# Feed-forward products as 32-column matmuls, placed behind the first and second weighted sums of a burst step

## The chip, the cores and the metric

One core of one Trainium2 chip. The metric is the device time of one execution in microseconds. The engines are named as in the profile: PE (TensorE, its weight loads are PEld), DVE (VectorE), ACT (ScalarE), POOL (GpSimd) and SP (SyncE, which issues the DMAs).

## What is computed

A stack of four blocks over x of 32 items, 256 tokens and 128 features: an attention with biases, a feed-forward of two experts out of eight, an attention without biases, and the same feed-forward again. Each block is a residual on a layer norm.

```python
def _L0_ffn_ref(x, gate_w, down_w, down_b, up_w, up_b):
    pooled = x.mean(axis=1)
    gate = softmax(pooled @ gate_w.T)
    top_w, top_i = top_k(gate, 2)                       # two experts for each item
    top_w = top_w / (top_w.sum(axis=-1, keepdims=True) + 1e-08)
    Wd, bd, Wu, bu = down_w[top_i], down_b[top_i], up_w[top_i], up_b[top_i]
    h = gelu(einsum('bsd,bkcd->bksc', x, Wd) + bd[:, :, None, :])
    h = h * top_w[:, :, None, None]
    out = einsum('bksc,bkdc->bsd', h, Wu)
    return out + (top_w[:, :, None] * bu).sum(axis=1)[:, None, :]

x = x + attn_a(layernorm(x))      # 16 heads of 8 features, biases, two masked scores
x = x + ffn(layernorm(x))
x = x + attn_b(layernorm(x))      # 16 heads of 8 features
x = x + ffn(layernorm(x))
```

## The kernel before

Everything stays on the chip between the blocks. A "turn" is one item in one of the two halves of the stack, so there are 64 turns. A software pipeline runs steps n from -6 to 70, each cut into eight parts p, and every engine has its own list of work for (n, p), the functions `step` in the blocks of the engines. In step n the scores of turn n + 2 are made and their maxima found ("scores", `max_side`, L789; the maximum by DVE at L598), the scores of turn n are made again the other way round and put through the exponential ("exps", `exp_side`, L803; ACT at L669), turn n's probabilities meet the values (`weigh`, L774, four groups g of four heads, 32 columns each, which fill the 128 output partitions side by side), turn n - 1 is transposed and projected, and the norms of turns n + 5 and n - 3 are made.

The names of the lines on PE are: L898 query and key projection, L920 value projection, L910 transpose of the weighted sums, L931 transpose of o, L943 transposes of the normalised x, L959 output projection, L886 transpose of the maxima.

The feed-forward of four turns, a group, is done in one "burst step"; there are 16, listed in `BURSTS` (19, 23, 27, 31, 35, 39, 43, 47, 49, 51, 54, 56, 58, 62, 66, 70). `down` (L815) multiplies the four normalised items with their expert weights, ACT applies Gelu (L722, with a table load before it at L713, and another one back to the exponential's table before L669), `up` (L830 for the bias in three bf16 parts, L838 for the product, fp32) makes the second product, and DVE adds it to x in two halves (L629, semaphore `added`). An fp32 matmul of the program shows as two matmuls in the trace.

PE's list of a burst step, in order: part 3: scores 3, exps 2 and 3, L910, `weigh` 0; part 4: scores 4, `down`, L920; part 5: scores 5, exps 4, `up`, L931, exps 5, `weigh` 1; part 6: scores 6, L943, exps 6; part 7: scores 7, `weigh` 2, exps 7, L959; `weigh` 3 follows in part 1 of the next step.

Scores, exps, `down` and `up` share three PSUM pairs in a ring. The order in which they take them is written out by hand in `uses`: scores 3, exps 3, down, scores 4, exps 4, up, scores 5, exps 5, scores 6 and so on, and each waits in `fill_pair` until the use three places earlier has been read: by DVE's maximum for scores, by ACT's exponential for exps, by the four Gelus for down, by DVE's two adds for up. So scores 5 take the place of scores 4, exps 5 that of exps 4, scores 6 that of up. ACT's list in a burst step is: the exponential of exps 3, the Gelu's table load, four Gelus, the copy of the values (L733), the table load back, the exponential of exps 4. DVE's list in part 5 is: the maximum of scores 5, statistics (L529), the two adds, in some steps the gate's weights for a batch (L561 to L577), aggregates (L538); then the maximum of scores 6. Each engine works through its list in order.

Of the kernel before, what the change touches and what calls it, by code (L numbers as in the profile page):

```python
# [13 lines left out]
P = 128  # L14
ITEMS, TOKENS, WIDTH = 32, 256, 128
TILES = TOKENS // P
# [20 lines left out]
GROUP = 4  # L37
DEEP = 2 * GROUP
GROUPS, PER_GROUP = 4, 4
SHARES, IN_SHARE = 2, 2  # L40
SUMS = HEAD + 1

# [13 lines left out]
def build(nc, x_dram_in, attn_w, attn_b, gate_w, down_w, down_b, up_w, up_b, tail_c, ident_c, iota_c, pick_c, out):  # L56
    ctx = ExitStack()
    with ctx:
        def sb(name, shape, dt=FP32):
            return ctx.enter_context(nc.sbuf_tensor(name, shape, dt))  # L60

        def sem(name):
            return ctx.enter_context(nc.semaphore(name))
# [3 lines left out]
        normT = sb("normT", [P, ITEMS, TOKENS])  # L67
# [58 lines left out]
        biasu_parts = [sb(f"biasu_parts{i}", [3 * ITEMS, WIDTH], BF16) for i in range(2)]  # L126
        pick = sb("pick", [3 * ITEMS, ITEMS], BF16)
        index = [sb(f"index{i}", [1, DEEP * TOP], U32) for i in range(2)]
        wd = [sb(f"wd{i}", [P, TOP, HIDDEN]) for i in range(DEEP)]
        wu = [sb(f"wu{i}", [P, WIDTH]) for i in range(DEEP)]  # L130
        hT = [sb(f"hT{i}", [P, TOKENS]) for i in range(GROUP)]
# [82 lines left out]
        def tensor_opening(pe):  # L214
            pe.wait_ge(weights_ready, 1)
# [14 lines left out]
        for group, burst in enumerate(BURSTS):  # L230
            for j in range(GROUP):
                turn = group * GROUP + j
# [11 lines left out]
        def group_at(n):  # L244

            return BURSTS.index(n) if n in BURSTS else None
# [10 lines left out]
        def live(turn):  # L257

            return 0 <= turn < TURNS
# [25 lines left out]
        down_done, h_ready = sem("down_done"), sem("h_ready")  # L285
# [19 lines left out]
        def fill_pair(pe, *use):  # L305

            if place[use] < 3:
                return
            kind, of, p = uses[place[use] - 3]
            if kind == "scores":  # L310
                pe.wait_ge(max_done, of * PAIRS + p + 1)
            elif kind == "exps":
                pe.wait_ge(exp_done, of * PAIRS + p + 1)
            elif kind == "down":
                pe.wait_ge(h_ready, (of + 1) * GROUP)
            else:
                pe.wait_ge(added, (of + 1) * 2)
# [18 lines left out]
        with nc.Block() as block:  # L336
# [424 lines left out]
            def _(pe):  # L761
                tensor_opening(pe)

                def weigh(turn, g):

                    pe.wait_ge(exp_done, turn * PAIRS + PER_GROUP // 2 * (g + 1))
                    if g == 0:
                        pe.wait_ge(v_ready, turn + 1)
                        if turn > 0:
                            pe.wait_ge(oT_ready, (turn - 1) + 1)  # L770
                    a, g2 = divmod(g, IN_SHARE)
                    for k in range(TILES):
                        for c in range(PER_GROUP):
                            last = nc.tensor.matmul(values_bank[32 * c:32 * (c + 1), a * TOKENS:(a + 1) * TOKENS],  # L774
                                                    values[turn % RING][:, k, PER_GROUP * g + c, :], probs[g % 2][:, c, k, :],
                                                    start=(g2 == 0 and k == 0), stop=(g2 == IN_SHARE - 1 and k == TILES - 1),
                                                    skip_group_check=True)
                    last.then_inc(pv_done, 1)
# [29 lines left out]
                def down(group):  # L808

                    fill_pair(pe, "down", group, 0)  # L810
                    pe.wait_ge(wd_ready, (group + 1) * GROUP)
                    bank = pair_of("down", group, 0)
                    for j in range(GROUP):
                        turn = group * GROUP + j
                        nc.tensor.matmul(bank[:, j // 2, (j % 2) * TOKENS:(j % 2 + 1) * TOKENS],  # L815
                                         wd[turn % DEEP][:, :, :].rearrange("p a b -> p (a b)"), normT[:, turn % ITEMS, :],
                                         start=(j % 2 == 0), stop=(j % 2 == 1), skip_group_check=True).then_inc(down_done, 1)

                def up(group):

                    b = batch_of(group * GROUP)
                    fill_pair(pe, "up", group, 0)
                    pe.wait_ge(split_done, SPLITS * (b + 1))
                    pe.wait_ge(wu_ready, (group + 1) * GROUP)
                    for half in range(2):
                        bank = pair_of("up", group, 0)[:, half, :]
                        for j in range(2):
                            turn = group * GROUP + 2 * half + j
                            col = turn - BATCHES[b][0]
                            nc.tensor.matmul(bank[:, j * TOKENS:(j + 1) * TOKENS].rearrange("p (t d) -> p t d", t=TILES),  # L830
                                             pick[:, col:col + 1].broadcast_to([3 * ITEMS, P]),
                                             biasu_parts[b % 2][:, :].unsqueeze(1).broadcast_to([3 * ITEMS, TILES, WIDTH]),
                                             start=(j == 0), stop=False, skip_group_check=True)
                        for j in range(2):
                            pe.wait_ge(h_ready, group * GROUP + 2 * half + j + 1)
                            for t in range(TILES):
                                at = j * TOKENS + t * P
                                last = nc.tensor.matmul(bank[:, at:at + P], hT[2 * half + j][:, t * P:(t + 1) * P],  # L838
                                                        wu[(group * GROUP + 2 * half + j) % DEEP][:, :],
                                                        start=False, stop=(j == 1 and t == TILES - 1), skip_group_check=True)  # L840
                        last.then_inc(up_done, 1)

                def logits(b):
# [27 lines left out]
                def step(pe, n, p):  # L871
# [8 lines left out]
                    if p == 1 and live(n + 1):  # L880
# [3 lines left out]
                        for t in range(TILES):  # L884
                            at = t * 6 * PAIRS
                            last = nc.tensor.transpose(m_bank[:, :].bitcast(BF16)[:, t * P:(t + 1) * P],  # L886
                                                       mparts[(n + 1) % 2][:, at:at + P], identb[:, :])
# [5 lines left out]
                    if p == 2 and live(n + 4):  # L893
# [3 lines left out]
                        for a, wmat in enumerate((wq, wk)):  # L897
                            last = nc.tensor.matmul(m_bank[:, a * TOKENS:(a + 1) * TOKENS], wmat, xnT[(n + 4) % 2][:, :],  # L898
                                                    start=(a == 0), stop=(a == 1), skip_group_check=True)
# [4 lines left out]
                    if p == 3 and live(n - 1):  # L904
                        fill_m(pe, o_ready, (n - 1) + 1)
                        pe.wait_ge(oT_ready, (n - 1) + 1)
                        for t in range(TILES):
                            for a in range(SHARES):
                                at = (t * SHARES + a) * P
                                last = nc.tensor.transpose(m_bank[:, at:at + P], oT[(n - 1) % 2][:, a, t * P:(t + 1) * P], ident[:, :])  # L910
                        last.then_inc(on_done, 1)
                    if p == 3 and live(n):
                        weigh(n, 0)
                    if p == 4 and group_at(n) is not None:
                        down(group_at(n))
                    if p == 4 and live(n + 3):
                        wv = projections[(n + 3) // ITEMS][2]
                        fill_m(pe, v_ready, (n + 3) + 1)
                        for t in range(TILES):
                            last = nc.tensor.matmul(m_bank[:, t * P:(t + 1) * P], xnT[(n + 3) % 2][:, t * P:(t + 1) * P], wv,  # L920
                                                    start=(t == 0), stop=(t == TILES - 1), skip_group_check=True)
                        last.then_inc(v_done, 1)
                    if p == 5 and live(n):
                        exp_side(n, 4)
                    if p == 5 and group_at(n) is not None:
                        up(group_at(n))
                    if p == 5 and live(n - 1):
                        fill_m(pe, onT_ready, (n - 1) + 1)
                        pe.wait_ge(o_ready, (n - 1) + 1)
                        for t in range(TILES):  # L930
                            last = nc.tensor.transpose(m_bank[:, t * P:(t + 1) * P], o[:, t, :], ident[:, :])  # L931
# [2 lines left out]
                        exp_side(n, 5)  # L934
                    if p == 5 and live(n):
                        weigh(n, 1)
                    if p == 6 and (live(n + 5) or live(n - 3)):
                        fill_m(pe, *((yT_ready, (n - 3) + 1) if live(n - 3) else (xnT_ready, (n + 5) + 1)))
                        pe.wait_ge(xy_ready, norm_steps(n))
                        for m in range(0 if live(n + 5) else 1, 2 if live(n - 3) else 1):  # L940
                            for t in range(TILES):
                                at = (m * TILES + t) * P
                                last = nc.tensor.transpose(m_bank[:, at:at + P], xy[(n + 5) % 2][:, m, t, :], ident[:, :])  # L943
                        last.then_inc(xyT_done, 1)
# [8 lines left out]
                    if p == PAIRS - 1 and live(n - 1):  # L953
# [4 lines left out]
                        for t in range(TILES):  # L958
                            last = nc.tensor.matmul(m_bank[:, t * P:(t + 1) * P], onT[:, t * P:(t + 1) * P], wo,  # L959
                                                    start=(t == 0), stop=(t == TILES - 1), skip_group_check=True)  # L960
# [51 lines left out]
```

## Time and profile before

| | us |
|---|---|
| median of 3 runs | 992.39 (991.34 to 994.3) |
| span of the profiled execution | 987.4 |
| PE busy | 917.8 |
| DVE busy | 787.2 |
| ACT busy | 772.6 |
| POOL busy | 666.2 |

The profiled execution is read by its span, from its first to its last instruction; the runs are timed from outside and are 5.0 us longer at the median. A row of the timeline gives the start from the span's beginning, the time until the last instruction of the row ended, the engine, the line of the kernel, the operation, the tiles (written from read), the shapes and the number of instructions, and in square brackets how long the engine stood idle before it and who released it. Rows of PE overlap, since a matmul's recorded end lies behind the start of the next one.

### The profile page before, as it was taken

The numbers are of one execution on the slowest core, as the hardware profiler recorded it, in microseconds if no ns is written. First come the engines' busy times: TensorE is split into PE (matmuls) and PEld (weight loads), VectorE is DVE, ScalarE is ACT, GpSimd is POOL, SyncE is SP. The second block draws the span as 40 slices with busy tenths as digits, with TensorE's granted clock in tenths as the row PEclk, the third lists the DMA queues.
The fourth block names the chain that finished last, engine by engine and source line by source line (L and its number), as shares of the span: only waits on it lengthen the run. The fifth ranks groups of instructions, "written<-read, shape, count | busy, mean of one in ns | idle before, by whom it ended". The sixth has DMA issues, their size and how long they took to land.

```text
span 987.4 us, 27821 instructions
## 1 busy us (share of the span) xinstructions
PE 917.8 (93%) x10286; PEld 513.9 (52%) x10286; DVE 787.2 (80%) x1394; ACT 772.6 (78%) x1299; POOL 666.2 (67%) x1280
## 2 busy tenths in 40 slices
PE   2589999999999999999999999999999998999885
PEld 1345555545555555555655555555555555654544
DVE  1688888898888888888788887888788878778524
ACT  2168888888888888888888888888888877887863
POOL 8465666667775886768676786768687585764442
PEclk9899999999999999999999999999999999999987
DMA  6577555444444443444444343444444454344001
GB/s 183 150 219 204 154 149 168 141 152 142 135 140 121 150 134 120 145 121 146 119 138 149 121 143 119 153 119 128 136 136 142 125 153 123 118 137 135 5 22 43
DMA packets 144694, 131.66 MB, mean 133 GB/s; under 512 B 9616, under 2 KB 127536, under 8 KB 144432
## 3 DMA queue, kind: packets, MB, share of 16 engines
q1 hardware_dynamic: 143456, 128.49, 43.8%
q8 instruction: 82, 1.34, 0.6%
q10 hardware_dynamic: 1104, 1.41, 0.5%
q14 instruction: 52, 0.43, 0.1%
HBM read 73.76 MB, written 55.57 MB: 131 GB/s over the span
## 4 chain that ended last, share of the span: by engine, by line
PE 67%; ACT 10%; DVE 9%; POOL 5%; issue 4%; DMA 3%; SPq 1%; POOLq 1%; ACTq 1%; DVEq 0%
PE values_bank L774 21%; PE ring L789 11%; PE ring L803 10%; PE m_bank L898 6%; DVE nmax L598 5%; PE m_bank L910 4%; PE m_bank L959 3%; PE m_bank L943 3%; PE m_bank L920 3%; ACT probs L669 2%; PE m_bank L931 2%; ACT hT L722 2%; ACT L713 2%; DMA k_stack<-scratch 2%; DMA scratch<-parts 1%
## 5 line engine op out<-in xcount | busy, mean ns | idle before, releaser
L598 DVE TENSOR_REDUCE nmax<-ring 128x4 f32<-128x1024 f32 x512 | 605.1, 1219 | 98.0 <-PE ring L789 97.0
L669 ACT ACTIVATE probs<-ring 128x1024 f32<-128x1024 f32 x512 | 518.2, 1025 | 54.8 <-PE ring L803 50.4
L774 PE MATMUL values_bank<-probs,values 128*32 128x256 f32 x4096 | 274.9, 386 | 0.7 <-ACT probs L669 0.6
L789 PE MATMUL ring<-k_stack,q_stack 64*128 64x256 bf16 x2048 | 201.2, 277 | 22.7 <-DMA k_stack<-scratch 18.6
L489 POOL TENSOR_SCALAR xy<-x,mv,rstd 128x128 f32<-128x128 f32 x256 | 200.6, 793 | 7.9
L803 PE MATMUL ring<-q_stack,k_stack 64*128 64x256 bf16 x2048 | 189.4, 273 | 8.5 <-DVE nmax L598 7.2
L774 PEld LDWEIGHTS values_bank<-probs,values 128*32 128x32 f32 x4096 | 107.1, 109 | 89.8 <-issue 37.2
L413 POOL TENSOR_SCALAR mparts<-nmax 128x32 bf16<-128x32 f32 x64 | 13.9, 217 | 188.0 <-DVE nmax L598 187.8
L789 PEld LDWEIGHTS ring<-k_stack,q_stack 64*128 64x128 bf16 x2048 | 70.3, 95 | 132.0 <-issue 56.0
L803 PEld LDWEIGHTS ring<-q_stack,k_stack 64*128 64x128 bf16 x2048 | 78.0, 94 | 93.9 <-issue 52.0
L511 POOL TENSOR_TENSOR parts<-rest,parts 128x512 bf16<-128x512 f32 x64 | 74.1, 1158 | 5.4
L505 POOL TENSOR_TENSOR rest<-qk,parts 128x512 f32<-128x512 f32 x64 | 74.1, 1158 | 5.4
L482 POOL TENSOR_TENSOR rstd<-varp,minus_half 128x4 f32<-128x4 f32 (+1 forms) x72 | 69.4, 964 | 6.0
L529 DVE BATCH_NORM_STATS2 raw<-x 128x6 f32<-128x128 f32 x256 | 60.9, 280 | 10.8 <-DMA x<-in_x 10.7
L586 DVE TENSOR_TENSOR x<-x,m_bank 128x256 f32<-128x256 f32 x64 | 27.0, 421 | 49.9 <-PE m_bank L959 49.9
L733 ACT COPY values<-m_bank 128x128 f32<-128x128 f32 x128 | 29.1, 282 | 42.3 <-PE m_bank L920 42.3
L943 PE MATMUL m_bank<-ident,xy 128*128 128x128 f32 x256 | 44.9, 294 | 12.3 <-ACT wb L193 9.0
L696 ACT COPY oT<-values_bank 128x512 f32<-128x512 f32 x64 | 37.4, 585 | 20.1 <-PE values_bank L774 19.0
L502 POOL TENSOR_SCALAR parts<-qk 128x512 bf16<-128x512 f32 x64 | 39.5, 618 | 18.8 <-ACT qk L706 17.2
L746 ACT COPY xnT<-m_bank 128x256 f32<-128x256 f32 x64 | 23.8, 372 | 31.0 <-PE m_bank L943 30.8
L910 PE MATMUL m_bank<-ident,oT 128*128 128x128 f32 x256 | 41.9, 286 | 2.5 <-ACT oT L696 0.8
L508 POOL TENSOR_SCALAR parts<-rest 128x512 bf16<-128x512 f32 x64 | 39.5, 618 | 5.9
(102 smaller groups left out, 1084.0 us busy)
## 6 DMA issues: line engine op xcount, KB each, us to landing
q_stack<-scratch SPq DMA_DIRECT2D x128, 256.0 KB
k_stack<-scratch SPq DMA_DIRECT2D x128, 256.0 KB
scratch<-parts SPq DMA_DIRECT2D x128, 192.0 KB, 2.2
scratch<-parts SPq DMA_DIRECT2D x128, 128.0 KB, 2.2
scratch<-parts SPq DMA_DIRECT2D x128, 64.0 KB, 2.4
out<-x SPq DMA_DIRECT2D x16, 256.0 KB, 2.7
x<-in_x SPq DMA_DIRECT2D x3, 768.0 KB, 7.3
q_stack<-maxT SPq DMA_DIRECT2D x128, 12.0 KB
```

The lines of the kernel that those rows point to most:

```text
L482: nc.gpsimd.tensor_tensor(rstd[i][:, both, :], varp[i][:, both, :], minus_half[:, both, :], ALU.pow).then_inc(rstd_done, 1)
L489: last = nc.gpsimd.tensor_scalar(xy[i][:, m, t, :], x[:, (turn % ITEMS) * TILES + t, :], mv[i][:, m, t, 0:1], rstd[i][:, m, t:t + 1], ALU. ...
L505: nc.gpsimd.tensor_tensor(rest[i][:, :, :], qk32[i][:, :, :], parts[i][:, 0], ALU.subtract).then_inc(rest_done, 1)
L511: nc.gpsimd.tensor_tensor(parts[i][:, 2], rest[i][:, :, :], parts[i][:, 1], ALU.subtract).then_inc(parts_ready, 1)
L529: last = nc.vector.bn_stats(raw[i][:, t, :], x[:, (turn % ITEMS) * TILES + t, :])
L598: nc.vector.tensor_reduce(dst, src, axis=AX.X, op=ALU.max, negate=True).then_inc(max_done, 1)
L669: nc.scalar.activation(probs[g % 2][:, c:c + 2, :, :], pair_of("exps", n, p)[:, :, :].rearrange("p x (k q) -> p x k q", k=TILES), ACT.Exp) ...
L774: last = nc.tensor.matmul(values_bank[32 * c:32 * (c + 1), a * TOKENS:(a + 1) * TOKENS], values[turn % RING][:, k, PER_GROUP * g + c, :], ...
L789: last = nc.tensor.matmul(pair_of("scores", turn, p)[:, a, t * TOKENS:(t + 1) * TOKENS], q_stack[z][rows, p, t * P:(t + 1) * P], k_stack[z ...
L803: last = nc.tensor.matmul(pair_of("exps", turn, p)[:, a, k * TOKENS:(k + 1) * TOKENS], k_stack[r][rows, p, k * P:(k + 1) * P], q_stack[r][ ...
L910: last = nc.tensor.transpose(m_bank[:, at:at + P], oT[(n - 1) % 2][:, a, t * P:(t + 1) * P], ident[:, :])
L943: last = nc.tensor.transpose(m_bank[:, at:at + P], xy[(n + 5) % 2][:, m, t, :], ident[:, :])
```

## The change

`by_columns` issues one product as four matmuls, each with 32 columns of the stationary operand and 32 partitions of the output. `down` and `up` use it for all their matmuls. In PE's list `down` moves from part 4 (behind scores 4) to the end of part 3, behind `weigh` 0, and `up` from part 5 (behind exps 4) to the end of part 5, behind `weigh` 1 and so right ahead of scores 6. `uses`, and with it the ring, and the lists of the other engines are as before.

```diff
--- before.py
+++ after.py
@@ -37,6 +37,7 @@
 GROUP = 4
 DEEP = 2 * GROUP
 GROUPS, PER_GROUP = 4, 4
+QUADS, QUAD = 4, 32
 SHARES, IN_SHARE = 2, 2
 SUMS = HEAD + 1
 
@@ -761,6 +762,13 @@
             def _(pe):
                 tensor_opening(pe)
 
+                def by_columns(out, stationary, moving, start, stop):
+
+                    for c in range(QUADS):
+                        at = slice(QUAD * c, QUAD * (c + 1))
+                        last = nc.tensor.matmul(out[at], stationary[:, at], moving, start=start, stop=stop, skip_group_check=True)
+                    return last
+
                 def weigh(turn, g):
 
                     pe.wait_ge(exp_done, turn * PAIRS + PER_GROUP // 2 * (g + 1))
@@ -812,9 +820,9 @@
                     bank = pair_of("down", group, 0)
                     for j in range(GROUP):
                         turn = group * GROUP + j
-                        nc.tensor.matmul(bank[:, j // 2, (j % 2) * TOKENS:(j % 2 + 1) * TOKENS],
-                                         wd[turn % DEEP][:, :, :].rearrange("p a b -> p (a b)"), normT[:, turn % ITEMS, :],
-                                         start=(j % 2 == 0), stop=(j % 2 == 1), skip_group_check=True).then_inc(down_done, 1)
+                        by_columns(bank[:, j // 2, (j % 2) * TOKENS:(j % 2 + 1) * TOKENS],
+                                   wd[turn % DEEP][:, :, :].rearrange("p a b -> p (a b)"), normT[:, turn % ITEMS, :],
+                                   start=(j % 2 == 0), stop=(j % 2 == 1)).then_inc(down_done, 1)
 
                 def up(group):
 
@@ -827,17 +835,17 @@
                         for j in range(2):
                             turn = group * GROUP + 2 * half + j
                             col = turn - BATCHES[b][0]
-                            nc.tensor.matmul(bank[:, j * TOKENS:(j + 1) * TOKENS].rearrange("p (t d) -> p t d", t=TILES),
-                                             pick[:, col:col + 1].broadcast_to([3 * ITEMS, P]),
-                                             biasu_parts[b % 2][:, :].unsqueeze(1).broadcast_to([3 * ITEMS, TILES, WIDTH]),
-                                             start=(j == 0), stop=False, skip_group_check=True)
+                            by_columns(bank[:, j * TOKENS:(j + 1) * TOKENS].rearrange("p (t d) -> p t d", t=TILES),
+                                       pick[:, col:col + 1].broadcast_to([3 * ITEMS, P]),
+                                       biasu_parts[b % 2][:, :].unsqueeze(1).broadcast_to([3 * ITEMS, TILES, WIDTH]),
+                                       start=(j == 0), stop=False)
                         for j in range(2):
                             pe.wait_ge(h_ready, group * GROUP + 2 * half + j + 1)
                             for t in range(TILES):
                                 at = j * TOKENS + t * P
-                                last = nc.tensor.matmul(bank[:, at:at + P], hT[2 * half + j][:, t * P:(t + 1) * P],
-                                                        wu[(group * GROUP + 2 * half + j) % DEEP][:, :],
-                                                        start=False, stop=(j == 1 and t == TILES - 1), skip_group_check=True)
+                                last = by_columns(bank[:, at:at + P], hT[2 * half + j][:, t * P:(t + 1) * P],
+                                                  wu[(group * GROUP + 2 * half + j) % DEEP][:, :],
+                                                  start=False, stop=(j == 1 and t == TILES - 1))
                         last.then_inc(up_done, 1)
 
                 def logits(b):
@@ -911,7 +919,7 @@
                         last.then_inc(on_done, 1)
                     if p == 3 and live(n):
                         weigh(n, 0)
-                    if p == 4 and group_at(n) is not None:
+                    if p == 3 and group_at(n) is not None:
                         down(group_at(n))
                     if p == 4 and live(n + 3):
                         wv = projections[(n + 3) // ITEMS][2]
@@ -922,8 +930,6 @@
                         last.then_inc(v_done, 1)
                     if p == 5 and live(n):
                         exp_side(n, 4)
-                    if p == 5 and group_at(n) is not None:
-                        up(group_at(n))
                     if p == 5 and live(n - 1):
                         fill_m(pe, onT_ready, (n - 1) + 1)
                         pe.wait_ge(o_ready, (n - 1) + 1)
@@ -934,6 +940,8 @@
                         exp_side(n, 5)
                     if p == 5 and live(n):
                         weigh(n, 1)
+                    if p == 5 and group_at(n) is not None:
+                        up(group_at(n))
                     if p == 6 and (live(n + 5) or live(n - 3)):
                         fill_m(pe, *((yT_ready, (n - 3) + 1) if live(n - 3) else (xnT_ready, (n + 5) + 1)))
                         pe.wait_ge(xy_ready, norm_steps(n))
```

## Rows read from the trace of the kernel before

**Rows 1.** The page: the span and its part 1, busy time of each engine.

```profile
span 987.4 us, 27821 instructions
...
PE 917.8 (93%) x10286; PEld 513.9 (52%) x10286; DVE 787.2 (80%) x1394; ACT 772.6 (78%) x1299; POOL 666.2 (67%) x1280
```

**Rows 2.** Timeline of PE in a plain step: start us, us, engine, line, operation.

```profile
351.64 1.07 PE L774 MATMUL values_bank<-probs,values 128*32 128x256 f32 x16
...
354.92 1.07 PE L774 MATMUL values_bank<-probs,values 128*32 128x256 f32 x16
```

**Rows 3.** Timeline of PE in the burst step at 364.62.

```profile
364.62 1.07 PE L774 MATMUL values_bank<-probs,values 128*32 128x256 f32 x16
365.62 0.39 PE L789 MATMUL ring<-k_stack,q_stack 64*128 64x256 bf16 x4
365.94 1.99 PE L815 MATMUL ring<-normT,wd 128*128 128x256 f32 x8
367.77 0.61 PE L920 MATMUL m_bank<-wa,xnT 128*128 128x128 f32 x4
368.31 0.39 PE L789 MATMUL ring<-k_stack,q_stack 64*128 64x256 bf16 x4
368.54 0.38 PE L803 MATMUL ring<-q_stack,k_stack 64*128 64x256 bf16 x4
368.87 0.39 PE L830 MATMUL ring<-biasu_parts,pick 96*128 96x256 bf16 x2
369.10 1.06 PE L838 MATMUL ring<-wu,hT 128*128 128x128 f32 x8
369.99 0.38 PE L830 MATMUL ring<-biasu_parts,pick 96*128 96x256 bf16 x2
...
371.11 0.38 PE L931 MATMUL m_bank<-ident,o 128*128 128x128 f32 x2
371.54 0.39 PE L803 MATMUL ring<-q_stack,k_stack 64*128 64x256 bf16 x4
371.86 1.07 PE L774 MATMUL values_bank<-probs,values 128*32 128x256 f32 x16
372.87 0.39 PE L789 MATMUL ring<-k_stack,q_stack 64*128 64x256 bf16 x4
```

**Rows 4.** Timeline of ACT in the same burst step.

```profile
365.82 1.28 ACT L713 ACT_TABLE_LOAD   x1
...
367.23 1.59 ACT L722 ACTIVATE hT<-ring,biasd 128x256 f32<-128x256 f32 x4
...
368.70 0.45 ACT L733 COPY values<-m_bank 128x128 f32<-128x128 f32 x2
...
369.17 1.28 ACT L669 ACT_TABLE_LOAD   x1
...
370.46 1.02 ACT L669 ACTIVATE probs<-ring 128x1024 f32<-128x1024 f32 x1
```

**Rows 5.** Timeline of DVE in the same burst step.

```profile
366.06 1.23 DVE L598 TENSOR_REDUCE nmax<-ring 128x4 f32<-128x1024 f32 x1 [0.49 <-PE ring L789]
...
371.31 0.69 DVE L629 TENSOR_TENSOR x<-x,ring 128x512 f32<-128x512 f32 x1 [0.35 <-PE ring L838]
```

**Rows 6.** Timeline of DVE in the burst step at 307.49, after the adds.

```profile
314.99 0.20 DVE L561 TENSOR_SCALAR tsum<-e 8x1 f32<-8x1 f32 x1
...
316.97 1.20 DVE L598 TENSOR_REDUCE nmax<-ring 128x4 f32<-128x1024 f32 x1
```

**Rows 7.** Busy time of each engine in four stretches, PEclk the granted clock.

```profile
core 0: us, PE busy (x) PEld busy (x) DVE busy (x) ACT busy (x) POOL busy (x), PEclk, DMA share, GB/s
797.58:800.99 3.41, 3.41 (x52) 1.60 (x44) 3.17 (x9) 3.02 (x7) 3.20 (x4) 1.00 0.60 186
800.99:804.39 3.40, 1.94 (x26) 1.13 (x26) 2.66 (x4) 2.05 (x2) 2.57 (x10) 1.00 0.38 113
804.39:807.80 3.41, 3.41 (x27) 1.56 (x27) 0.72 (x2) 1.84 (x3) 3.29 (x4) 0.50 0.47 137
...
835.10:838.50 3.40, 2.19 (x25) 1.27 (x26) 3.40 (x4) 1.81 (x2) 0.92 (x4) 1.00 0.73 210
```

## The prediction

> **What bounds the kernel now.** I read the page first: the span is 987.4 us and TensorE (PE) is recorded busy for 93% of it, no other engine for more than 80% [rows 1]. As PE's ends are modelled, that share alone proves little, so I next read PE's timeline for a step without feed-forward work. From the start of the first weighted sum to that of the second it takes 354.92 - 351.64 = 3.28 us [rows 2], and the same sum of the next step starts at 364.62 [rows 3], 12.98 us after the one at 351.64, with PE rows one behind the other. A plain step is a queue of PE work without holes; whatever PE loses in it moves the end.
>
> Then the burst step at 364.62, in which a group of four items gets its feed-forward products. Call its first weighted sum w0, its second w1, the score products of the maximum side S4, S5, S6, those of the exponential side E4, E5, the two feed-forward products D (down) and U (up). From w0 to w1 it takes 371.86 - 364.62 = 7.24 us [rows 3], 3.96 more than in the plain step. D takes 367.77 - 365.94 = 1.83 us, U 371.11 - 368.87 = 2.24 us, 4.07 together: PE spends its extra time on the products themselves and hardly waits.
>
> Two other engines run a chain beside it. ScalarE (ACT) starts a table load at 365.82, then the four Gelus, the copy of the values, a second table load, and the exponential of E4, which ends at 370.46 + 1.02 = 371.48 [rows 4]. E5 starts at 371.54 [rows 3], 0.06 later: E5 needs the ring slot that this exponential empties. So the two chains are of equal length in a burst step, and U is just what fills PE until the exponential is done. VectorE (DVE) adds the second half of U to x from 371.31 to 372.00 [rows 5]; S6, which takes U's slot, starts at 372.87, long after, because E5 and w1 lie between.
>
> **The change part by part.** The profiled execution is 987.4 us and the median of the runs 992.4, so 5.0 us lie around the span; I add my sum to the median.
>
> Narrow products. Each product becomes four matmuls of 32 columns, and the work per product stays whole. w0 is such work already: 16 matmuls, four rounds of four side by side, next row 1.00 us later [rows 3]. The row itself lasts 1.07, of which 0.39 is the tail of one, so the last round starts at about 0.69 and a round takes 0.69 / 3 = 0.23 us. D today takes 1.83 / 8 = 0.23 us for one full-width matmul of the same 256 columns. So D costs the same. U's matmuls stream 128 columns; eight of them take 369.99 - 369.10 = 0.89 us, 0.11 each. No row shows four narrow ones with so few columns. The lower bound is 0.11 per round (the streamed columns are the same), the upper is a round of w0, 0.23. I take 0.11, since in w0 too the round costs what the full-width matmul of its length does. It is 20 rounds, so 2.2 us against up to 4.6.
>
> Changes of the array's shape. After w0's last round at 0.69 the next shape starts at 1.00, so 0.31 instead of 0.23: a change costs about 0.1 us. Before: w0, S4, D with the value projection, S5 with E4, U with the transpose of o, E5, w1, S6: seven changes. After: w0 with D, S4, the projection, S5 with E4, the transpose, E5, w1 with U, S6: seven again, because the projection and the transpose, with which D and U shared a shape, stay. Saved: nothing.
>
> D ahead of S4. Times from here are from w0's start, before in brackets, from [rows 3] less 364.62. D starts at 0.69 + 0.23 = 0.91 and its last round at 0.91 + 7 x 0.22 = 2.45. S4 starts 0.31 later, at 2.76 (1.00). Its maximum starts 366.06 - 365.62 = 0.44 after it and takes 1.23 [rows 5], so it ends at 4.43. The projection still starts near 3.1 (3.15). But S5 takes S4's slot and so waits for that maximum: 4.48 (3.69). E4 follows 0.23 later at 4.71 (3.92) and ends, with a row of 0.38, at 5.09 (4.30). PE stands some 0.9 us ahead of S5. D's other readers gain nothing: the Gelus run behind the first table load without a hole [rows 4], so an earlier D doesn't start them earlier.
>
> U out of the gap. On ACT all is as before up to the copy of the values, which ends at 368.70 + 0.45 = 369.15, or 4.53. The second table load stands in ACT's order behind the wait for E4. Before, E4 ended at 4.30 and the copy set the start; after, E4 does, at 5.12 (4.55). If the load didn't wait, this shift would be zero; the trace can't tell, as both were done, so the bounds are 0 and 0.57. I take 0.57, by program order. The exponential ends 1.29 + 1.02 later at 7.43, E5 starts at 7.48 (6.92), w1 at 7.80 (7.24). PE has by then only the transpose to do after E4, some 0.4 us, and stands for about 2.2 us. Before, U ran in it.
>
> U ahead of S6. U starts at 7.80 + 0.91 = 8.71, its last of 20 rounds at 8.71 + 19 x 0.11 = 10.80. The last add starts about 0.32 after the last matmul (371.31 against the transpose's start at 371.11 less one round) and takes 0.69 [rows 5]. S6 needs U's slot: 10.80 + 0.32 + 0.69 + 0.05 = 11.86. Before, it started at 372.87, or 8.25. **So a burst step grows by 3.6 us**, or 3.0 if the table load doesn't wait. I take 3.55. Nothing behind gives it back, as the steps that follow are full PE queues [rows 2].
>
> This holds where S6 exists, in the bursts of steps 19 to 58: thirteen of sixteen. 13 x 3.55 = 46 us (13 x 3.0 = 39 at least). In the burst of step 62 U behind w1 loses cover too, about 1 us; in the last two there is nothing between the parts, 0.
>
> Small VectorE operations. In five bursts (19, 27, 35, 43, 51) DVE makes the gate's weights between the adds and S6's maximum: from 314.99 to 316.97, 1.98 us [rows 6]. After, that series starts only when S6 is released, so S6's maximum is up to 1.98 - 0.49 = 1.5 us late, and E7 and the next E0 need the ring. Part of the lag exists today. Bounds 0 and 1.5, I take 0.9: 5 us.
>
> The granted clock. From 802.3 PE waited for POOL; in the stretch 800.99 to 804.39 it was busy 1.94 of 3.40 us at full clock, and from 804.39 to 807.80 the granted clock was 0.50, that is 1.2 instead of 2.4 GHz; PE got 27 matmuls done there against 52 in the 3.41 us from 797.58 at 1.00 [rows 7]. Such a fall costs up to 3.41 x (1 - 27/52) = 1.6 us. In another stretch, 835.10 to 838.50, PE was busy 2.19 us and the clock of that stretch stayed at 1.00. The burst step after the change leaves PE with about 0.9 us of work between the projection (3.6) and E5 (7.48), more idle than the stretch ahead of the fall. So I expect a fall in most of the thirteen, on E5, w1 and U, partly on waits where it is free: ten at 1.3 us, 13 us. Bounds: none, and thirteen at 1.6, 21 us.
>
> Other queues. SyncE and POOL keep their orders. D asks for the expert weights that POOL copied a step earlier. The stores and the statistics of the second pass wait for the adds; they come some 3.6 us later, as PE's own step does.
>
> Sum: 46 + 1 + 5 + 13 = 65 us; 992.4 + 65 = 1057, and I say 1056.
>
> **The rivals.** (1) The two waits appear but the clock holds: 46 + 1 + 5, so 1044. For it: a wait of PE around 835 left it at 1.00 [rows 7]. (2) The narrow rounds of U don't run at 0.11 but at 0.23: 20 x 0.12 = 2.4 us in thirteen bursts, 31 more: 1087. For it: no row shows such rounds; against it: w0's equality with D. (3) Not slower: the shape changes are dear and the waits don't come. Each change costs 0.1 us by [rows 3]; if D and U each saved the one in and the one out, 4 x 0.1 x 16 = 6 us: 986. It decides if the exponential of E4 has ended when PE reaches E5, at about 5.2 after w0 instead of 7.43. Against it stand ACT's busy 5.66 us from 365.82 to 371.48, which no order of PE shortens, and the count of seven and seven.
>
> The Trainium skill ("TensorEngine Tiling (Array Packing)", Key Properties) says that changing the tiling mode drains TensorE, which speaks for putting D and U beside the narrow weighted sums. The row agrees that a change costs something, 0.1 us. It would give rival (3) only if changes were saved.
>
> (4) A smaller loss: the table load doesn't wait, the gate's lag is hidden, the clock holds: 39, so 1031.
>
> **How the numbers follow.** Forecast 0.60, rival (1) 0.20, (2) 0.10, (4) 0.06, (3) 0.04. The forecast with both ends of the clock and the table load runs from 1040 to 1072; with (1) and most of (4) the range is 1032 to 1072, which leaves out (2), (3) and the rest. About 0.3% is what a measurement of this kernel can tell from no change. Only (3) is faster, or, half fulfilled, the same: faster 0.02, same 0.02, slower 0.96.
>
> **What would show it.** In a burst step after the change: w0 to w1 still above 7.2 us though U is gone from it; PE idle ahead of S5 until a maximum ends, ahead of E5 until an exponential ends (2 us), ahead of S6 until VectorE's second add ends (about 0.9 us); w1 to S6 near 4.1 us instead of 1.01; the clock at 0.50 in some of these steps. Wrong if E5 starts some 5 us after w0, if U takes well over 2.3 us, or if the following steps get shorter than 12.98.

## The result and the profile after

| | median us | ratio to before, 95% interval |
|---|---|---|
| before | 992.49 | |
| after | 1066.45 (1065.54 to 1067.69) | 1.0766 (1.0744 to 1.0787) |

The change costs 74 us. The prediction was 1056 (1032 to 1072).

The page of the changed kernel: the span, the busy times, and the granted clock in forty slices. The answering lines of before are in [rows 1].

```profile
span 1064.6 us, 30509 instructions
...
PE 945.7 (89%) x11630; PEld 522.6 (49%) x11630; DVE 787.9 (74%) x1394; ACT 772.7 (73%) x1299; POOL 667.1 (63%) x1280
...
PEclk9899999999999999999999999999899998999986
```

PE works 28 us more than before by its records and is still busy for a smaller share of the span. Apart from the start and the end of the span, the clock shows 8 in two slices of the later half.

PE's timeline of the burst step that answers [rows 3]: start, us, line, operation, and in brackets the idle time and who ended it. PE's line numbers are eight higher than before, those of the other engines one; L769 is the new helper, that is `down` (written from normT) and `up` (from the bias parts and wu).

```profile
372.00 1.07 PE L782 MATMUL values_bank<-probs,values 128*32 128x256 f32 x16
372.89 1.91 PE L769 MATMUL ring<-normT,wd 128*32 128x256 f32 x32
374.73 0.39 PE L797 MATMUL ring<-k_stack,q_stack 64*128 64x256 bf16 x4
375.05 0.71 PE L928 MATMUL m_bank<-wa,xnT 128*128 128x128 f32 x4
376.45 0.39 PE L797 MATMUL ring<-k_stack,q_stack 64*128 64x256 bf16 x4 [0.68 <-DVE nmax L599]
376.68 0.38 PE L811 MATMUL ring<-q_stack,k_stack 64*128 64x256 bf16 x4
376.99 0.44 PE L937 MATMUL m_bank<-ident,o 128*128 128x128 f32 x2
379.52 0.61 PE L811 MATMUL ring<-q_stack,k_stack 64*128 64x256 bf16 x4 [2.09 <-ACT probs L670]
380.05 1.93 PE L782 MATMUL values_bank<-probs,values 128*32 128x256 f32 x16
381.76 0.66 PE L769 MATMUL ring<-biasu_parts,pick 96*32 96x256 bf16 x8
...
383.52 1.05 PE L769 MATMUL ring<-wu,hT 128*32 128x128 f32 x32
385.39 0.39 PE L797 MATMUL ring<-k_stack,q_stack 64*128 64x256 bf16 x4 [0.82 <-DVE x L630]
...
386.84 1.07 PE L782 MATMUL values_bank<-probs,values 128*32 128x256 f32 x16
```

Three brackets stand where before there was none. Scores 5 (376.45) wait 0.68 us for VectorE's maximum of scores 4. Exps 5 (379.52) wait 2.09 us for ScalarE's exponential of exps 4. Scores 6 (385.39) wait 0.82 us for VectorE's second add. (The prediction had 0.9, 2.2 and 0.9 us.) And the second weighted sum, at 380.05, takes 1.71 us until `up` starts, where the first, at 372.00, takes 0.89 until `down` does.

The other two engines in the same step, ScalarE (ACT) and VectorE (DVE), to be read against [rows 4] and [rows 5]:

```profile
373.21 1.28 ACT L714 ACT_TABLE_LOAD   x1
...
374.61 1.55 ACT L723 ACTIVATE hT<-ring,biasd 128x256 f32<-128x256 f32 x4
376.04 0.47 ACT L734 COPY values<-m_bank 128x128 f32<-128x128 f32 x2
377.14 1.28 ACT L670 ACT_TABLE_LOAD   x1 [0.64 <-PE ring L811]
378.44 1.02 ACT L670 ACTIVATE probs<-ring 128x1024 f32<-128x1024 f32 x1
```

```profile
375.16 1.23 DVE L599 TENSOR_REDUCE nmax<-ring 128x4 f32<-128x1024 f32 x1 [2.21 <-PE ring L797]
...
384.65 0.69 DVE L630 TENSOR_TENSOR x<-x,ring 128x512 f32<-128x512 f32 x1 [0.41 <-PE ring L769]
```

From the first table load (373.21) to the end of the copy (376.51) ScalarE works without a hole, 3.30 us against 3.33 before. The second table load then waits 0.64 us for exps 4, as its bracket says. VectorE's last add starts at 384.65 and ends 0.05 us ahead of scores 6.

What PE waited for in the whole execution, with the sum, the count and the longest wait:

```profile
PE ring L811 <- ACT probs L670: 27.2, 13, 2.1
...
PE ring L797 <- DVE x L630: 10.6, 13, 0.8
...
PE ring L797 <- DVE nmax L599: 9.6, 15, 0.7
```

Two of the three waits come thirteen times, once in each burst step that has scores 6; the third comes in them too, and twice elsewhere.

The clock of that burst step: busy time of each engine in three stretches, PEclk the granted clock.

```profile
core 0: us, PE busy (x) PEld busy (x) DVE busy (x) ACT busy (x) POOL busy (x), PEclk, DMA share, GB/s
375.84:379.25 3.41, 0.98 (x10) 0.51 (x10) 2.17 (x4) 2.76 (x5) 1.54 (x2) 1.00 0.74 187
379.25:382.66 3.41, 3.14 (x40) 1.70 (x44) 0.00 (x0) 1.60 (x3) 0.00 (x0) 0.50 0.47 136
382.66:386.08 3.42, 2.60 (x75) 2.11 (x68) 1.92 (x7) 0.00 (x0) 0.00 (x0) 1.00 0.00 0
```

PE was busy for 0.98 us of the first stretch, and the next one, with exps 5, the second weighted sum and the beginning of `up`, was granted 0.50, that is 1.2 GHz. In the trace's clock records this happens in all thirteen burst steps, nine times for 3.41 us and four times for 6.83 us, 58.0 us together.

### The profile page after: what moved, and what is told of

Read it like the earlier page. It is cut to its first block, busy times and chain, and to the rows that moved or that the text cites. A ratio compares the mean times of both kernels' runs of the same rounds, so it can differ in the third digit from the quotient of the medians.

```text
span 1064.6 us, 30509 instructions
## 1 busy us (share of the span) xinstructions
PE 945.7 (89%) x11630; PEld 522.6 (49%) x11630; DVE 787.9 (74%) x1394; ACT 772.7 (73%) x1299; POOL 667.1 (63%) x1280
## 4 chain that ended last, share of the span: by engine, by line
PE 71%; DVE 11%; ACT 6%; POOL 5%; issue 3%; DMA 2%; POOLq 1%; ACTq 1%; SPq 0%; DVEq 0%
PE values_bank L782 22%; PE ring L797 11%; PE ring L811 10%; PE ring L769 8%; DVE nmax L599 7%; PE m_bank L906 5%; PE m_bank L918 3%; PE m_bank L967 3%; PE m_bank L951 3%; PE m_bank L928 2%; ACT probs L670 2%; PE m_bank L937 2%; ACT L670 2%; DMA k_stack<-scratch 1%; PE m_bank L894 1%
## 5 line engine op out<-in xcount | busy, mean ns | idle before, releaser
L782 PE MATMUL values_bank<-probs,values 128*32 128x256 f32 x4096 | 284.2, 396 | 0.6 <-ACT probs L670 0.6
L811 PE MATMUL ring<-q_stack,k_stack 64*128 64x256 bf16 x2048 | 191.2, 275 | 39.2 <-ACT probs L670 27.2
L630 DVE TENSOR_TENSOR x<-x,ring 128x512 f32<-128x512 f32 x32 | 22.0, 688 | 91.1 <-PE ring L769 91.1
L769 PE MATMUL ring<-wu,hT 128*32 128x128 f32 x1024 | 47.5, 344 | 0.0
```

Source lines behind the costliest of these rows:

```text
L769: last = nc.tensor.matmul(out[at], stationary[:, at], moving, start=start, stop=stop, skip_group_check=True)
L811: last = nc.tensor.matmul(pair_of("exps", turn, p)[:, a, k * TOKENS:(k + 1) * TOKENS], k_stack[r][rows, p, k * P:(k + 1) * P], q_stack[r][ ...
```

## The experiments

All are edits of the changed kernel. "w0 to w1" is the time from the first to the second weighted sum of a burst step, "w1 to w2" from the second to the third, in a burst step in which the clock held, the commonest value of the thirteen (the changed kernel has steps in which it held from w0 to w1, but none in which it held from w1 to w2). "At half clock" is the sum of the stretches at 0.50 in the thirteen burst steps. Each ratio is to runs of the kernel before that were taken beside the experiment; their medians were 990.8 us for the first four experiments, 991.4 for the next three and 990.0 for the last.

| kernel | median us | ratio to before, 95% interval | w0 to w1 | w1 to w2 | at half clock, us |
|---|---|---|---|---|---|
| before | | | 7.33 | 2.45 | 0 |
| after | 1066.45 | 1.0766 (1.0744 to 1.0787) | 7.84 | | 58.0 |
| full width at the new places | 1062.03 | 1.0724 (1.0701 to 1.0748) | 8.04 | 5.64 | 41.0 |
| narrow at the old places | 989.12 | 0.9989 (0.9976 to 1.0003) | 7.37 | 2.45 | 0 |
| only `down` moved | 996.58 | 1.0058 (1.0036 to 1.0081) | 7.98 | 2.45 | 0 |
| only `up` moved | 1053.99 | 1.0632 (1.0608 to 1.0657) | 7.33 | 5.52 | 44.4 |
| after, wait filled | 1039.61 | 1.0491 (1.0473 to 1.0508) | 7.84 | 5.53 | 0 |
| after, ring order | 1020.06 | 1.0287 (1.0270 to 1.0304) | 5.57 | 5.59 | 0 |
| after, no table loads | 1028.72 | 1.0364 (1.0338 to 1.0389) | 6.56 | 5.52 | 17.1 |
| full width, wait filled | 1043.35 | 1.0546 (1.0509 to 1.0582) | 8.04 | 5.64 | 0 |

The clock fell in all thirteen burst steps of the changed kernel, in ten at full width, in twelve with only `up` moved, in five without the table loads, and in none of the others.

**Full width at the new places.**

```diff
-                    for c in range(QUADS):
-                        at = slice(QUAD * c, QUAD * (c + 1))
-                        last = nc.tensor.matmul(out[at], stationary[:, at], moving, ...)
-                    return last
+                    return nc.tensor.matmul(out, stationary, moving, ...)
```

> The products at their new places, each again one full-width matmul instead of four of 32 columns. Theory: the loss comes from the places alone (waits of PE ahead of scores 5, exps 5 and scores 6, and the fallen clock), and the width costs nothing; two more changes of the array's shape per burst step (weighted sums to full width), 0.1 us each, in part on waits: 1066 to 1070 us. Rival: the narrow form is what costs (four times the instructions, or rounds that don't run side by side): then most of the 74 us go, 1000 to 1035 us.

1062.0 us, a little below what the theory said and far above the rival. The places make the loss, not the width. That it came out below the changed kernel instead of slightly above had another cause, which the last experiment shows: its burst steps spent 41.0 us at half clock instead of 58.0.

**Narrow at the old places.**

```diff
-                    if p == 3 and group_at(n) is not None:
+                    if p == 4 and group_at(n) is not None:
                         down(group_at(n))
...
                         exp_side(n, 4)
+                    if p == 5 and group_at(n) is not None:
+                        up(group_at(n))
...
                         weigh(n, 1)
-                    if p == 5 and group_at(n) is not None:
-                        up(group_at(n))
```

> The narrow matmuls alone, at the places of the kernel before. Theory: the rounds cost what the full-width matmuls cost; two more changes of the array's shape per burst step, about 0.2 us in thirteen to sixteen steps, of which 0.1 lies on the wait ahead of exps 5: 992 to 996 us, and no fall of the clock in the burst steps. Rival (the narrow form costs): 1030 us and more.

No measurable difference: the interval holds 1. Four times the matmul instructions cost nothing that shows in the time, and rounds of 128 columns run at full speed: in the changed kernel the last eight rounds of `up` begin at 383.52 and their row ends 1.05 us later, as L838's eight matmuls did in 1.06 [rows 3].

**Only `down` moved.** The second half of the edit above, without the first.

> Narrow, only the down product moved behind the first weighted sum; up stays between exps 4 and exps 5. Theory: scores 5 wait for the maximum of scores 4, 0.8 us per burst step, exps 4 come 0.8 us later, but up still fills the wait ahead of exps 5, and scores 6 don't wait for the adds: w0 to w1 near 8.1 us, w1 to w2 as before at 2.45, 0.8 to 1.0 us in thirteen steps, 1003 to 1006 us, no fall of the clock. Rival (down's place is half of the whole loss): 1030 us.

996.6 us, less than expected. PE's timeline of a burst step:

```profile
365.36 1.07 PE L782 MATMUL values_bank<-probs,values 128*32 128x256 f32 x16
...
369.80 0.39 PE L797 MATMUL ring<-k_stack,q_stack 64*128 64x256 bf16 x4 [0.68 <-DVE nmax L599]
...
370.34 0.40 PE L769 MATMUL ring<-biasu_parts,pick 96*32 96x256 bf16 x8
...
373.34 1.07 PE L782 MATMUL values_bank<-probs,values 128*32 128x256 f32 x16
```

The wait ahead of scores 5 is there with the same 0.68 us. `up` (370.34) still fills the time until the exponential is done, and there is no other wait. It costs 7.98 - 7.33 = 0.65 us per burst step, 8.5 us in thirteen; 5.8 us stand in the medians. The expectation took 0.8 us or more for each step and 992.5 us for the kernel before, which ran at 990.8 beside this experiment.

**Only `up` moved.** The first half of that edit, without the second.

> Narrow, only the up product moved behind the second weighted sum; down stays behind scores 4. Theory: w0 to w1 stays near 7.3 us although up has left, since exps 5 wait for the exponential of exps 4; up and the wait for the adds then lie bare between w1 and scores 6, 3.1 us in thirteen steps, 40 us, plus 4 for the gate's weights, plus 10 to 20 for falls of the clock, as PE stands 2.5 us ahead of exps 5: 1046 to 1057 us. Without falls of the clock 1037 us. Rival (both moves are needed for the loss): below 1020 us.

1054.0 us, as expected. PE's timeline:

```profile
372.86 1.07 PE L782 MATMUL values_bank<-probs,values 128*32 128x256 f32 x16
...
377.42 0.44 PE L937 MATMUL m_bank<-ident,o 128*128 128x128 f32 x2
379.76 0.39 PE L811 MATMUL ring<-q_stack,k_stack 64*128 64x256 bf16 x4 [1.91 <-ACT probs L670]
...
385.83 0.39 PE L797 MATMUL ring<-k_stack,q_stack 64*128 64x256 bf16 x4 [0.81 <-DVE x L630]
```

The time from w0 to w1 is unchanged at 7.33 although 2.2 us of PE work have left it: the wait ahead of exps 5, 1.91 us, has taken their place, and `up` with the wait for the adds lies bare behind w1. So `up` is most of the loss, and either move alone loses.

**The wait filled.**

```diff
+                    if p == 5 and group_at(n) is not None and live(n + 2):
+                        pe.wait_ge(h_ready, (group_at(n) + 1) * GROUP)
+                        for _ in range(FILLERS):
+                            nc.tensor.matmul(pair_of("up", group_at(n), 0)[:, 0, :]..., identb[:, :],
+                                             identb[:, :].unsqueeze(1).broadcast_to([P, 4, P]), start=True, stop=True, ...)
                     if p == 5 and live(n):
                         exp_side(n, 5)
```

> The changed kernel, with eight more full-width bf16 matmuls of 512 columns per burst step (about 0.21 us each, 1.7 us together) in PE's wait ahead of exps 5; they write to up's PSUM pair, which up overwrites, and change no output. Theory: they fit into the 2.1 us of wait and so cost nothing, but keep the granted clock at 1.00, so what is left is the waits alone: 992.5 + 46 + 4 + 1, 1040 to 1050 us. Rival (the 20 us over the waits aren't the clock's): 1066 us or, if the fillers don't fit, more.

1039.6 us: 27 us less than the changed kernel, for eight matmuls more in each of thirteen steps. PE's timeline, with the fillers at L943:

```profile
369.41 1.07 PE L783 MATMUL values_bank<-probs,values 128*32 128x256 f32 x16
...
373.86 0.39 PE L798 MATMUL ring<-k_stack,q_stack 64*128 64x256 bf16 x4 [0.68 <-DVE nmax L600]
...
374.68 1.89 PE L943 MATMUL ring<-identb 128*128 128x512 bf16 x8
376.93 0.39 PE L812 MATMUL ring<-q_stack,k_stack 64*128 64x256 bf16 x4 [0.36 <-ACT probs L671]
377.25 1.07 PE L783 MATMUL values_bank<-probs,values 128*32 128x256 f32 x16
378.14 0.40 PE L770 MATMUL ring<-biasu_parts,pick 96*32 96x256 bf16 x8
...
381.32 0.39 PE L798 MATMUL ring<-k_stack,q_stack 64*128 64x256 bf16 x4 [0.81 <-DVE x L631]
...
382.78 1.07 PE L783 MATMUL values_bank<-probs,values 128*32 128x256 f32 x16
```

The three waits are where they were, the one ahead of exps 5 now 0.36 us besides 1.89 us of fillers; w0 to w1 is 7.84, w1 to w2 5.53 in each of the thirteen steps, and the clock is at 1.00 throughout them. What is left, 48 us, is the price of the waits, with some 5 us for the gate's weights and step 62 in it; what went is the price of the clock.

**Ring order.** `uses` takes `up` one place later.

```diff
-        DOWN_AFTER, UP_AFTER = 3, 4
+        DOWN_AFTER, UP_AFTER = 3, 5
```

> The changed kernel with up one place later in the ring's order, behind exps 5 instead of exps 4. Now scores 5 wait for the Gelus, exps 5 for the maximum of scores 4, up for the exponential of exps 4, scores 6 for the maximum of scores 5, scores 7 for the adds. Theory (the waits are those of the ring): the second weighted sum starts some 2 us earlier, 5.3 us after the first, up starts at 7.5 instead of 8.7, scores 6 at 9.8 instead of 11.9 (before: 8.25), 1.5 to 1.7 us in thirteen steps and fewer falls of the clock: 1012 to 1025 us. Rival (the loss lies in the place of the products, whatever the ring): 1060 us and more.

1020.1 us, inside what was expected. PE's timeline:

```profile
369.37 1.07 PE L782 MATMUL values_bank<-probs,values 128*32 128x256 f32 x16
...
373.59 0.39 PE L797 MATMUL ring<-k_stack,q_stack 64*128 64x256 bf16 x4 [0.45 <-ACT hT L723]
...
374.82 1.07 PE L782 MATMUL values_bank<-probs,values 128*32 128x256 f32 x16
376.65 0.40 PE L769 MATMUL ring<-biasu_parts,pick 96*32 96x256 bf16 x8 [0.76 <-ACT probs L670]
...
378.96 0.39 PE L797 MATMUL ring<-k_stack,q_stack 64*128 64x256 bf16 x4
...
380.41 1.07 PE L782 MATMUL values_bank<-probs,values 128*32 128x256 f32 x16
```

The second weighted sum starts 5.45 us after the first in this step; here scores 5 wait for a Gelu (0.45), `up` for the exponential (0.76), scores 6 (378.96) follow `up` without a wait. Same products at the same places, and 29 us of loss instead of 74, or instead of the 48 us of the filled kernel, in which the clock doesn't fall either: the waits are those of the ring. In this order later waits appear, which I didn't foresee: w2 to w3 grows from 3.06 to 3.59 us, and in the five steps with the gate's weights to 5.20 us, against 4.32 in the changed kernel.

**No table loads.**

```diff
-                        nc.scalar.activation(spare[:, group:group + 1], bqs[:, :], ACT.Gelu)
+                        nc.scalar.activation(spare[:, group:group + 1], bqs[:, :], ACT.Exp)
...
-                            nc.scalar.activation(hT[j][:, :], src, ACT.Gelu, bias=biasd[run][:, col:col + 1])...
+                            nc.scalar.activation(hT[j][:, :], src, ACT.Exp, bias=biasd[run][:, col:col + 1])...
```

> The changed kernel with Exp in place of Gelu, so that no table is loaded in a burst step; the hidden activations of the feed-forward differ by that. Theory: ACT's chain of table loads, Gelus and copy sets the start of exps 5; without the two loads the exponential of exps 4 starts as soon as exps 4 are done, at 5.1 instead of 6.4 us after the first weighted sum, so w0 to w1 is near 6.5 us, 1.3 us less in thirteen steps, 17 us, and with a wait of 0.8 instead of 2.1 us the clock falls less often, 0 to 20 us more: 1029 to 1049 us. Rival (exps 5 wait for something else): 1066 us.

1028.7 us, at the low end. ScalarE's exponential of exps 4, and what PE waited for:

```profile
373.46 1.02 ACT L670 ACTIVATE probs<-ring 128x1024 f32<-128x1024 f32 x1 [0.91 <-PE ring L811]
```

```profile
PE ring L797 <- DVE x L630: 10.6, 13, 0.8
PE ring L811 <- ACT probs L670: 10.6, 13, 0.8
```

Now no table load stands between exps 4 and their exponential, which starts as soon as PE has made exps 4 (ScalarE waits 0.91 us for them): w0 to w1 is 6.56, 1.28 less, the length of one table load. The wait ahead of exps 5 sums to 10.6 instead of 27.2 us, and the clock falls in five burst steps instead of thirteen. ScalarE's chain does set exps 5.

**Full width, wait filled.** The fillers and the full-width helper together.

> The same eight fillers in PE's wait ahead of exps 5, with the products at the new places as full-width matmuls. With full-width products unfilled, those burst steps in which the clock held took 8.04 + 5.64 us from the first to the third weighted sum, against 7.84 + 5.53 with narrow ones and fillers, 0.31 us more. Theory (narrow products behind a weighted sum do save two changes of the array's shape per burst step, and the lower total of the unfilled full-width kernel came from fewer falls of the clock): 0.31 us in thirteen steps, 4 us above the filled narrow kernel, 1042 to 1046 us, no fall of the clock. Rival (full width is the cheaper form): 1036 us or less.

1043.4 us, as expected. With the clock out of the way the full-width products cost 0.20 us more from w0 to w1 and 0.11 more from w1 to w2, 4 us in thirteen steps. PE's timeline, `down` and `up` at L768:

```profile
370.17 1.07 PE L780 MATMUL values_bank<-probs,values 128*32 128x256 f32 x16
371.17 1.99 PE L768 MATMUL ring<-normT,wd 128*128 128x256 f32 x8
...
378.20 1.07 PE L780 MATMUL values_bank<-probs,values 128*32 128x256 f32 x16
379.21 0.39 PE L768 MATMUL ring<-biasu_parts,pick 96*128 96x256 bf16 x2
```

`down` starts 1.00 us after the weighted sum instead of 0.89 and its row is 0.08 us longer (1.99 against 1.91); `up` starts 1.01 us after its weighted sum instead of 0.89. So the difference lies where the array goes from 32 columns to full width. That is what the narrow form was good for at these places: it spares two changes of the array's shape per step.

## Why the prediction was right, and where it was not

The places of the waits came out as worked, within 0.05 us, and their sizes nearly so. Measured from w0 in the burst step shown, with the worked value in brackets: `down` 0.89 (0.91), scores 4 2.73 (2.76), scores 5 4.45 (4.48), exps 4 4.68 (4.71), the table load 5.14 (5.12), the exponential's end 7.46 (7.43), exps 5 7.52 (7.48). The filled kernel gives the rest without the clock: w1 7.84 (7.80), scores 6 at 381.32 - 369.41 = 11.91 (11.86). The two bounds that I had to choose between are settled: the table load does wait for exps 4 (its bracket of 0.64 us), and a narrow round of 128 columns takes 0.11 us.

- **Waits:** 46 us forecast; in the filled kernel (7.84 + 5.53) - (7.33 + 2.45) = 3.59 us per step, and over all thirteen 46.0 us.
- **The gate's weights:** 0.9 us in five steps forecast; w2 to w3 went from 3.50 to 4.32 us in them, 4.1 us together.
- **Step 62:** 1 us forecast; w0 to w2 grew from 8.33 to 9.01.
- **Shape changes:** counted as seven and seven, nothing saved; narrow products at the old places, where two changes come in, made no difference that can be measured, and the comparison at the new places prices two changes at 0.31 us, 0.20 at `down` and 0.11 at `up` (0.1 each was worked). The Trainium skill ("TensorEngine Tiling (Array Packing)", Key Properties) says that a change of the tiling mode drains TensorE. The 0.31 us agree with that, as a cost at each change; it is small here, 4 us against 46 of waits.
- **The clock: mis-sized.** The step that failed is "ten at 1.3 us, 13 us", with its upper bound of 21. It fell in thirteen of thirteen steps, in four of them for twice the time of the one fall in [rows 7], so 1.6 us was no bound for a fall. Against the filled kernel the changed one loses 27 us in the medians; in the times from w0 to w2 of its thirteen steps it loses 25.6, that is 0.44 us for each of the 58.0 us at half clock. The nine short falls cost 1.4 to 1.7 us each, near the bound, and the four long ones 2.7 to 2.9. Full width at the new places loses 17.5 us to 41.0, a ratio of 0.43.

Together 46 + 4 + 1 + 26 = 77 us, and the spans differ by 1064.6 - 987.4 = 77.2. The medians differ by 74, since 5.0 us lay around the profiled span before and 1.8 us (1066.42 - 1064.6) after.

The prediction's own terms add up to 1057 us, not 1056, and with the upper bounds of the clock (21) and of the gate's weights (5 x 1.5 = 7.5) to 992.4 + 46 + 1 + 7.5 + 21 = 1068; no sum written in it reaches its upper end of 1072. The measured 1066.45 lies near the upper end of what the terms allow: the waits were understood, and the clock took twice its forecast.

Rival (1), waits without the clock, did not come about in the changed kernel; the filled kernel shows what it would have been: 1044 forecast, 1039.6 measured. Rival (2) is out by the length of `up`'s rounds. Rival (3) is out since exps 5 wait for ScalarE's chain, as the run without table loads shows. Rival (4) fell with its first condition.

Left open: what decides between a fall of 3.41 and one of 6.83 us (in the changed kernel the four long ones began 6.3 to 6.8 us after w0, 0.7 us or more ahead of exps 5, and the nine short ones at 7.1 us or later; at full width the two long ones began at 6.5 and 6.7 us and the short ones at 7.4 or later, with only `up` moved the long one at 6.5 and the short ones at 6.7 or later; but no run was made on that), and why full width had three burst steps (19, 39 and 51) without a fall. The fillers show that PE's idle time ahead of exps 5 brings the fall; no run tells how much idle time it takes. Nor is it explained why PE stood for 0.8 to 1.0 us inside `up`, with no releaser in the profile, in the burst step 51 of the two narrow kernels that have `up` at its old place (w0 to w1 8.79 and 9.20 us there). A version clearly faster than the kernel before was not found; in its thirteen burst steps no single wait of PE is over 0.5 us.

## What to carry to other kernels

Work that looks misplaced on the bound engine may be what fills its wait for another engine: before moving it, find the buffer that the next instruction needs, and who empties it how late. When such a wait opens on TensorE, the clock may fall for the work behind it (in 13 of 13 steps with a wait of 2.1 us here, in 5 of 13 with 0.8 us), so price both; where the wait can't be removed, a few matmuls that write to a buffer which is overwritten anyway gave back 27 of 74 us here. Saving changes of the array's shape (0.1 to 0.2 us each here) pays only if no wait of that size is opened.

## What the runs showed of the hardware

The granted clock fell in every one of thirteen steps after a wait of 2.1 us in a sparse stretch (PE busy 0.98 of 3.41 us in the step shown), and the work behind it lost 0.43 to 0.48 us per us at 1.2 GHz (17.5 of 41.0 us at full width, 25.6 of 58.0 in the changed kernel, 8.1 of 17.1 without the table loads). Four matmuls of 32 columns side by side cost TensorE the same as one of 128, 0.22 us a round of 256 streamed fp32 columns and 0.11 us a round of 128, although they are four instructions instead of one. Going from 32 columns to full width behind a weighted sum cost 0.20 us at `down` and 0.11 us at `up`. A table load of 1.28 us waited for the same matmuls as the exponential that it serves, so taking it away made w0 to w1 1.28 us shorter.
